# An SSM mixer stage: the carried part of y computed feature-major, with C times the decays formed on GpSimd

## The chip, the cores and the metric

The kernel runs on one core of one Trainium2 chip. The metric is the device time of one execution in microseconds. A core has TensorE (PE, with its weight loads shown as PEld), VectorE (DVE), ScalarE (ACT), GpSimd (POOL) and SyncE (SP), which run their own instruction streams and meet only at semaphores; DMA queues are fed by SP and by POOL.

## The reference, cut to what matters

The program is a two-layer block: attention and a mixture of experts, then a state-space mixer (an SSM in chunked form) and a second mixture of experts. The change touches the mixer alone. Its core, per batch element and head (64 heads of 64 features, state size 128):

```python
proj = input_states @ in_proj_w.T          # gate z, x with B and C, dt
hBC  = silu(conv1d_causal_4_taps(x, B, C) + bias)
dt   = softplus(dt + dt_bias);  Adt = -exp(A_log) * dt
A_cum = cumsum(Adt within a chunk)
Y_diag = (C @ B^T * exp(segsum(Adt))) @ (x * dt)            # inside a chunk
states = B^T @ (exp(A_cum[-1] - A_cum) * x * dt)            # of each chunk
state carried into chunk c = exp(chunk decay) * earlier state + states
Y_off[l, p] = sum_n C[l, n] * carried[p, n] * exp(A_cum[l]) # carried part
y  = Y_diag + Y_off + D * x
out = (rmsnorm(y * silu(gate)) * norm_w) @ out_proj_w.T
```

The kernel uses chunks of its own, four of 128 tokens in a batch element of 512, so three chunks have a carried part.

## The kernel before, in words

**Tiles.** The mixer loops over 4 batch elements (`GROUPS`) and, in each, 32 tiles of 128 features (two heads each): 128 tiles, one a step. Features lie on the partitions, the 512 tokens of the batch element along the free dimension. `mixer_stream` (L2063) runs the steps; a step works on five tiles at once, `tiles[0]` the newest to `tiles[4]` the oldest, so one tile passes through five steps. The order of the work on each engine is written out by hand in one function for each engine, and only semaphore waits tie them.

**One step, engine by engine, before the change.**
- TensorE (L2139 on): project x of tile 0 into PSUM (`project`, L2148, 6 matmuls); transpose the convolved x of tile 1 (L2162); for y of tile 3, transpose back the scaled carried part `y_off` (L2171) and add the inside-the-chunk products (L2176, two heads side by side in the two halves of the array); project z of tile 0 (L2148 again); state sums of tile 1 (L2189); C times states of tile 2 into bank `PO` (L2197); output projection of tile 4 (L2204).
- ScalarE: scale `PO` of tile 3 by the decays into `y_off` (L2230, 6 small instructions); eight Relu on `l_mat` of tile 1 (L2239); first tap of the convolution of tile 0 (`cv`, L2245); Exp of `l_mat` (L2251); square of tile 4 (L2256); tanh for x (`thx`, L2261) and for z (`thg`, L2266) of tile 0.
- VectorE: the carried states of tile 2, a copy (L2288) and four multiply-adds (L2293); the decay matrix times C B^T for tile 2 (L2341, both inputs in SBUF, shown as `outs<-l_mat,g_mat`); `xdt` of tile 1 out of PSUM (L2305); three taps of tile 0 (L2315); `yd` of tile 3 (L2322); the SiLU product `xc` of tile 0 (L2328, both inputs in SBUF); `sgt` of tile 0 (L2334).
- GpSimd: `xdec`, the decayed x, of tile 1 (L2368, waits for `xdt`); running sum of squares for tile 4 (L2376, shown as `gates<-gates,sq`); `yg` of tile 3 (L2383).

**What is woven in.** While batch element b is in the mixer, the routing of batch element b-1 for the second mixture of experts runs inside steps 4 to 15 of b (`route_pe`, `route_act`, `route_dve`, `route_pool`: 12 steps with extra work, called through `route(...)` at the marked places). From step 16 of b GpSimd also issues, behind its own step, scatters to HBM (`route_scatter`, L1680 to L1683: two tiny copies and an indirect DMA): two a step in four steps, then one a step in 12 steps, and one a step in the first four steps of the next b (of the drain after the last). Between two batch elements each engine runs a `between` part (the norm). This is so for b = 1, 2, 3; b = 0 has neither.

```python
for it in range(first, FT // U):
    for u in range(U):
        run(b, it, u)
        n = (it - first) * U + u
        for m in range(n + min(n, U), n + 1 + min(n + 1, U)):
            scatter(en, b - 1, m)
```

## Time and profile before

| what | value |
|---|---|
| runs shown | 2289.25, 2297.69, 2305.37 us (median 2297.69) |
| profiled execution, own time | 2296.97 us |
| its span | 2295.2 us |
| mixer steps (first to last `thx`, L2261) | 870.1 to 1931.8 us of the span |
| busy over the span | PE 1986.1, PEld 1622.4, DVE 1700.5, ACT 1461.2, POOL 973.7 us |
| steps of b = 1 with scatters, 1270 to 1410 us | PE 140.00 of 140 us, DVE 128.15, ACT 123.41, POOL 98.04; granted clock 1.00 |
| routing steps and `between`, 1140 to 1270 us | PE 117.73 of 130 us, DVE 115.00, ACT 99.89, POOL 59.91; granted clock 0.93 |

A row of the timeline gives start in us from the span's start, time in us, engine, line, operation, what is written and read, shapes, how many instructions are merged, and in brackets how long the engine was idle before it and who ended that. Instructions of ScalarE and VectorE overlap a little at their ends, so the distance between two starts is the cost of the first in a full queue, and less than its duration.

### The profile page before, as it was taken

The numbers are of one execution on the slowest core, as the hardware profiler recorded it, in microseconds if no ns is written. First come the engines' busy times: TensorE is split into PE (matmuls) and PEld (weight loads), VectorE is DVE, ScalarE is ACT, GpSimd is POOL, SyncE is SP. The second block draws the span as 40 slices with busy tenths as digits, with TensorE's granted clock in tenths as the row PEclk, the third lists the DMA queues.
The fourth block names the chain that finished last, engine by engine and source line by source line (L and its number), as shares of the span: only waits on it lengthen the run. The fifth ranks groups of instructions, "written<-read, shape, count | busy, mean of one in ns | idle before, by whom it ended". The sixth has DMA issues, their size and how long they took to land.

```text
span 2295.2 us, 40993 instructions
## 1 busy us (share of the span) xinstructions
PE 1986.1 (87%) x12211; PEld 1622.4 (71%) x12211; DVE 1700.5 (74%) x3913; ACT 1461.2 (64%) x3983; POOL 973.7 (42%) x1025
## 2 busy tenths in 40 slices
PE   4787988887699468999998998999989999689995
PEld 4566766666677256888877887878877788467772
DVE  4676766676634667999899998999989997664444
ACT  1473747465244157888887888878887887345550
POOL 0120302021177112455454765547655567177550
PEclk8799989899699779999999999999999999899998
DMA  4147383837833403444343554445534452635557
GB/s 129 38 152 295 130 350 106 338 109 282 328 97 102 147 10 138 158 154 145 127 147 125 169 175 144 142 137 171 165 137 142 146 179 93 214 117 176 162 146 272
DMA packets 143589, 372.67 MB, mean 162 GB/s; under 512 B 22256, under 2 KB 67696, under 8 KB 141072
## 3 DMA queue, kind: packets, MB, share of 16 engines
q1 hardware_dynamic: 128160, 328.39, 41.8%
q0 software_dynamic: 15216, 41.67, 5.3%
q8 instruction: 106, 1.74, 0.3%
q14 instruction: 107, 0.88, 0.1%
HBM read 232.71 MB, written 137.27 MB: 161 GB/s over the span
## 4 chain that ended last, share of the span: by engine, by line
PE 60%; DVE 17%; ACT 13%; issue 5%; DMA 2%; POOL 1%; SPq 1%; DVEq 0%; POOLq 0%; ACTq 0%
PE bank L2148 12%; PE bank L2204 6%; ACT work L701 5%; PE bank L2585 5%; PE bank L2176 4%; DVE cv L2315 3%; PE bank L2197 3%; PE bank L2189 3%; PE bank L1074 3%; PE bank L2622 2%; ACT l_mat L2239 2%; PE bank L2162 2%; DVE nmax L607 2%; PE bank L1103 2%; PE bank L775 1%
## 5 line engine op out<-in xcount | busy, mean ns | idle before, releaser
L2148 PE MATMUL bank<-h_hi,wi 128*128 128x512 f32 x1024 | 403.9, 436 | 1.3 <-ACTq L151 1.3
L2239 ACT ACTIVATE l_mat<-l_mat,cum_tok 128x128 f32<-128x128 f32 x1024 | 315.1, 424 | 0.0
L2315 DVE SCALAR_TENSOR_TENSOR cv<-bank,cw,cv 128x511 f32<-128x511 f32 (+2 forms) x384 | 287.4, 748 | 32.1 <-ACT cv L2245 13.5
L2368 POOL TENSOR_TENSOR xdec<-xdt,dec_tok 128x384 f32<-128x384 f32 x128 | 107.9, 843 | 387.6 <-DVE xdt L2305 354.4
L2383 POOL TENSOR_TENSOR yg<-yd,sgt 128x512 f32<-128x512 f32 x128 | 227.2, 1775 | 45.7 <-DVE yd L2322 45.7
L2204 PE MATMUL bank<-wo,yg 128*128 128x256 f32 x1024 | 242.5, 380 | 1.5 <-POOL yg L2383 1.5
L2148 PEld LDWEIGHTS bank<-h_hi,wi 128*128 128x128 f32 x1024 | 195.5, 191 | 62.0 <-issue 23.8
L2148 PE MATMUL bank<-h_lo,wi 128*128 128x512 f32 x512 | 203.4, 397 | 0.0
L2204 PEld LDWEIGHTS bank<-wo,yg 128*128 128x128 f32 x1024 | 185.1, 191 | 21.5 <-POOL yg L2383 1.9
L2376 POOL TENSOR_TENSOR gates<-gates,sq 128x512 f32<-128x512 f32 x128 | 164.1, 1282 | 72.0 <-ACT sq L2256 71.9
L845 POOL CAST w_hi<-w_raw 128x512 fp32r<-128x512 f32 x32 | 21.1, 659 | 392.0 <-ACTq L151 241.2
L701 ACT ACTIVATE work<-bank,nmax 128x512 f32<-128x512 f32 (+3 forms) x256 | 135.1, 535 | 68.7 <-DVE nmax L607 67.3
L2230 ACT ACTIVATE y_off<-bank,e_tok 128x64 f32<-128x64 f32 x768 | 170.8, 323 | 8.0 <-PE bank L2197 7.6
L2261 ACT ACTIVATE thx<-cv 128x512 f32<-128x512 f32 x128 | 80.8, 631 | 148.3 <-DVE cv L2315 148.3
L2341 DVE TENSOR_TENSOR outs<-l_mat,g_mat 128x1024 f32<-128x1024 f32 x128 | 157.9, 1234 | 0.0
L2693 POOL DMA_INDIRECT chosen_rows<-experts_held,experts_kept x127 | 121.5, 957 | 71.9 <-ACT experts_held L2673 57.9
L660 DVE TENSOR_TENSOR hb<-bank,pt_hi 128x512 fp32r<-128x512 f32 (+1 forms) x192 | 114.4, 600 | 50.5 <-ACT pt_hi L655 50.4
L2176 PE MATMUL bank<-outs,xdt 128*64 128x128 f32 x2048 | 144.4, 285 | 0.0
L607 DVE TENSOR_REDUCE nmax<-bank 128x1 f32<-128x512 f32 (+3 forms) x256 | 117.6, 484 | 31.2 <-PE bank L780 31.2
L2251 ACT ACTIVATE l_mat<-l_mat 128x1024 f32<-128x1024 f32 x128 | 137.3, 1073 | 0.0
L2176 PEld LDWEIGHTS bank<-outs,xdt 128*64 128x64 f32 x2048 | 112.8, 140 | 22.2 <-issue 22.2
L2293 DVE SCALAR_TENSOR_TENSOR st<-st,e_in,bank 128x64 f32<-128x64 f32 x512 | 121.0, 278 | 9.1
(419 smaller groups left out, 4947.6 us busy)
## 6 DMA issues: line engine op xcount, KB each, us to landing
sorted_rows<-blank SPq DMA_DIRECT2D x16, 4644.0 KB, 31.9
wi<-in_weights_split SPq DMA_DIRECT2D x128, 512.0 KB, 3.8
l_mat<-running_sums SPq DMA_DIRECT2D x128, 512.0 KB, 4.9
experts_got<-chosen_rows SPq DMA_DIRECT2D x32, 512.0 KB, 8.6
wo<-out_weights_normed SPq DMA_DIRECT2D x128, 128.0 KB
experts_xt<-sorted_rows SPq DMA_DIRECT2D x127, 129.0 KB, 2.3
w_raw<-in_wi SPq DMA_DIRECT2D x32, 256.0 KB, 2.7
in_weights_split<-w_hi SPq DMA_DIRECT2D x32, 256.0 KB, 2.9
```

Source lines behind the costliest of these rows:

```text
L607: last = e.tensor_reduce(nmax[:, h, q:q + 1], bank[n % 3][:, col:col + P * (q + 1)], AX.X, ALU.max, negate=True)
L701: last = e.activation(pp[:, h % 2, QOFF[q]:QOFF[q] + w], bank[u][:, col:col + w], ACT.Exp, bias=nmax[:, h, q:q + 1], accum_out=ssum[:, h, ...
L2148: mm = e.matmul(dst[:, :], l, r[:, k, tok], start=(n == 0), stop=(n == 3 * KD - 1))
L2176: mm = e.matmul(PY[rows, c * P:(c + 1) * P], xdt[:, w.four, c, rows], m_mat[:, w.two, hh, c * P:(c + 1) * P], start=False, stop=(c == NC - 1),
L2204: mm = e.matmul(token_major((bank[0], bank[1]), i), yg[:, w.two, i * P:(i + 1) * P], wo[:, w.two, :], start=False, stop=w.end, skip_group_ ...
L2230: last = e.activation(y_off[:, c, rows], PO[:, c * P + hh * SSM_P:c * P + (hh + 1) * SSM_P], ACT.Identity, scale=e_tok[:, c, hh, bass.ds(w ...
L2239: last = e.activation(part, part, ACT.Relu, bias=cum_tok[:, c, hh, bass.ds(w.g, 1)], scale=-1.0)
L2251: e.activation(l_mat[:, w.four, :, :], l_mat[:, w.four, :, :], ACT.Exp, scale=-1.0).then_inc(s_l, 1)
L2315: e.scalar_tensor_tensor(out=cv[:, w.two, n:SEQ], in0=PSX[w.two][:, 0:SEQ - n], scalar=cw[:, bass.ds(w.f, 1), TAPS - 1 - n], in1=cv[:, w.t ...
L2341: v.e.tensor_tensor(m_mat[:, w.two, :, :], l_mat[:, w.four, :, :], g_mat[:, w.b, :, :].rearrange("p c l -> p (c l)").unsqueeze(1).broadcas ...
L2376: e.tensor_tensor(sq_sum[:, w.b % 2, :], sq_sum[:, w.b % 2, :], sq[:, :], ALU.add).then_inc(s_acc, 1)
L2383: e.tensor_tensor(yg[:, w.two, :], yd[:, :], sgt[:, w.four, :], ALU.mult).then_inc(s_yg, 1)
```

## The change

The carried part of y is no longer made token-major, scaled and transposed back. ScalarE makes the exponential of the broadcast running sums for both heads (`ce`, 768 columns, tile 1) before its eight Relu, and waits for it because the Relu overwrite `l_mat`. GpSimd multiplies it by C (tile 2, right behind `xdec`), in three buffers. TensorE then adds states times `ce` to the same PSUM tile as the rest of y, six matmuls in pairs of heads; the three transposes and the three C-times-state matmuls go, with bank `PO` and `e_tok`. The first state is copied out of PSUM by ScalarE at the end of its step of tile 1, instead of by VectorE at the start of the next; VectorE waits for it (`s_first`) as well as for the state sums. The two tanh write straight into `xc` and `sgt`. On TensorE the routing work marked "p" moves behind a wait for the first tap of tile 0 (`s_cv`); on ScalarE that marked "a" comes first in the step.

```diff
--- before.py
+++ after.py
@@ -1428,14 +1427,13 @@
     start.close()
 
     cv = sb("cv", [P, 2, SEQ], where=stream)
-    thx, thg = sb("thx", [P, SEQ], where=stream), sb("thg", [P, SEQ], where=stream)
     xc = sb("xc", [P, U, SEQ], where=stream)
     sgt = sb("sgt", [P, U, SEQ], where=stream)
     l_mat = sb("l_mat", [P, U, 2, SEQ], where=stream)
     xdt = sb("xdt", [P, U, NC, P], where=stream)
     xdec = sb("xdec", [P, NC - 1, P], where=stream)
     st = sb("st", [P, 2, NC - 1, P], where=stream)
-    y_off = sb("y_off", [P, NC - 1, P], where=stream)
+    ce = sb("ce", [P, 3, 2, SEQ - P], where=stream)
     yd = sb("yd", [P, SEQ], where=stream)
     yg = sb("yg", [P, 2, SEQ], where=stream)
     sq = sb("sq", [P, SEQ], where=stream)
...
@@ -2157,7 +2154,7 @@
         w = tiles[1]
         if w.live:
             e.wait_ge(s_xc, done(w.g))
-            e.wait_ge(s_st, done(w.g - 1, 3))
+            e.wait_ge(s_st, done(w.g - 1, 2))
             for c in range(NC):
                 mm = e.transpose(PT[:, c * P:(c + 1) * P], xc[:, w.four, c * P:(c + 1) * P], ident[:, :])
             mm.then_inc(s_t, 1)
...
@@ -2165,16 +2162,20 @@
         if w.live:
             e.wait_ge(s_m, done(w.g))
             e.wait_ge(s_xdt, done(w.g))
-            e.wait_ge(s_offs, done(w.g))
+            e.wait_ge(s_ce, done(w.g))
+            e.wait_ge(s_st, done(w.g, 2))
             e.wait_ge(s_yd, done(w.g - 1))
-            for c in range(1, NC):
-                e.matmul(PY[:, c * P:(c + 1) * P], y_off[:, c - 1, :], ident[:, :], is_transpose=True, start=(c == 1),
-                         stop=False, skip_group_check=True)
             for c in range(NC):
                 for hh in range(2):
                     rows = slice(hh * SSM_P, (hh + 1) * SSM_P)
-                    mm = e.matmul(PY[rows, c * P:(c + 1) * P], xdt[:, w.four, c, rows],
-                                  m_mat[:, w.two, hh, c * P:(c + 1) * P], start=False, stop=(c == NC - 1),
+                    e.matmul(PY[rows, c * P:(c + 1) * P], xdt[:, w.four, c, rows],
+                             m_mat[:, w.two, hh, c * P:(c + 1) * P], start=(c == 0), stop=False,
+                             skip_group_check=True)
+            for c in range(1, NC):
+                for hh in range(2):
+                    rows = slice(hh * SSM_P, (hh + 1) * SSM_P)
+                    mm = e.matmul(PY[rows, c * P:(c + 1) * P], st[:, w.two, c - 1, rows],
+                                  ce[:, w.three, hh, (c - 1) * P:c * P], start=False, stop=(c == NC - 1),
                                   skip_group_check=True)
             mm.then_inc(s_y, 1)
         w = tiles[0]
...
@@ -2188,14 +2189,10 @@
             for c in range(NC - 1):
                 mm = e.matmul(PT[:, c * P:(c + 1) * P], b_tok[:, w.b, c, :], xdec[:, c, :], start=True, stop=True)
             mm.then_inc(s_ss, 1)
-        w = tiles[2]
+        w = tiles[0]
         if w.live:
-            e.wait_ge(s_st, done(w.g, 3))
-            e.wait_ge(s_offs, done(w.g - 1))
+            e.wait_ge(s_cv, done(w.g))
             route("p")
-            for c in range(NC - 1):
-                mm = e.matmul(PO[:, c * P:(c + 1) * P], c_t[:, w.b, c, :], st[:, w.two, c, :], start=True, stop=True)
-            mm.then_inc(s_off, 1)
         w = tiles[4]
         if w.live:
             e.wait_ge(s_yg, done(w.g))
...
@@ -2219,20 +2216,13 @@
 
     def mixer_act_step(a, tiles, route):
         e = a.e
-        w = tiles[3]
-        if w.live:
-            e.wait_ge(s_off, done(w.g))
-            route("a")
-            e.wait_ge(s_y, done(w.g - 1))
-            for c in range(NC - 1):
-                for hh in range(2):
-                    rows = slice(hh * SSM_P, (hh + 1) * SSM_P)
-                    last = e.activation(y_off[:, c, rows], PO[:, c * P + hh * SSM_P:c * P + (hh + 1) * SSM_P],
-                                        ACT.Identity, scale=e_tok[:, c, hh, bass.ds(w.g, 1)])
-            last.then_inc(s_offs, 1)
+        route("a")
         w = tiles[1]
         if w.live:
             e.wait_ge(s_lb[w.four], 16 + w.loaded_i)
+            e.wait_ge(s_y, done(w.g - 3))
+            e.activation(ce[:, w.three, :, :], l_mat[:, w.four, :, P:SEQ], ACT.Exp).then_inc(s_e, 1)
+            e.wait_ge(s_e, done(w.g))
             for hh in range(2):
                 for c in range(NC):
                     part = l_mat[:, w.four, hh, c * P:(c + 1) * P]
...
@@ -2257,13 +2247,18 @@
         w = tiles[0]
         if w.live:
             e.wait_ge(s_tap, done(w.g, 3))
-            e.wait_ge(s_xc, done(w.g - 1))
-            e.activation(thx[:, :], cv[:, w.two, :], ACT.Tanh, scale=0.5).then_inc(s_thx, 1)
+            e.wait_ge(s_yd, done(w.g - U))
+            e.activation(xc[:, w.four, :], cv[:, w.two, :], ACT.Tanh, scale=0.5).then_inc(s_thx, 1)
         w = tiles[0]
         if w.live:
             e.wait_ge(s_z, done(w.g))
-            e.wait_ge(s_sg, done(w.g - 1))
-            e.activation(thg[:, :], PSZ[:, :], ACT.Tanh, scale=0.5).then_inc(s_thz, 1)
+            e.wait_ge(s_yg, done(w.g - U))
+            e.activation(sgt[:, w.four, :], PSZ[:, :], ACT.Tanh, scale=0.5).then_inc(s_thz, 1)
+        w = tiles[1]
+        if w.live:
+            e.wait_ge(s_ss, done(w.g))
+            e.wait_ge(s_y, done(w.g - 2))
+            e.activation(st[:, w.two, 0, :], PT[:, 0:P], ACT.Copy).then_inc(s_first, 1)
 
     def mixer_act_between(a, b):
         e = a.e
...
@@ -2283,15 +2278,15 @@
         w = tiles[2]
         if w.live:
             e.wait_ge(s_ss, done(w.g))
+            e.wait_ge(s_first, done(w.g))
             route("a")
-            e.wait_ge(s_off, done(w.g - 2))
-            e.tensor_copy(st[:, w.two, 0, :], PT[:, 0:P]).then_inc(s_st, 1)
             for c in (1, 2):
-                e.wait_ge(s_st, done(w.g, 3) + (c - 3))
+                if c == 2:
+                    e.wait_ge(s_st, done(w.g, 2) - 1)
                 for hh in range(2):
                     cols = slice(hh * SSM_P, (hh + 1) * SSM_P)
                     last = e.scalar_tensor_tensor(out=st[:, w.two, c, cols], in0=st[:, w.two, c - 1, cols],
-                                                  scalar=e_in[:, hh, bass.ds(w.g, 1), c],
+                                                  scalar=e_in[:, hh, bass.ds(w.g, 1), c - 1],
                                                   in1=PT[:, c * P + hh * SSM_P:c * P + (hh + 1) * SSM_P],
                                                   op0=ALU.mult, op1=ALU.add)
                 last.then_inc(s_st, 1)
...
@@ -2324,14 +2319,12 @@
         w = tiles[0]
         if w.live:
             e.wait_ge(s_thx, done(w.g))
-            e.wait_ge(s_yd, done(w.g - U))
-            e.scalar_tensor_tensor(out=xc[:, w.four, :], in0=thx[:, :], scalar=1.0, in1=cv[:, w.two, :],
+            e.scalar_tensor_tensor(out=xc[:, w.four, :], in0=xc[:, w.four, :], scalar=1.0, in1=cv[:, w.two, :],
                                    op0=ALU.add, op1=ALU.mult).then_inc(s_xc, 1)
         w = tiles[0]
         if w.live:
             e.wait_ge(s_thz, done(w.g))
-            e.wait_ge(s_yg, done(w.g - U))
-            e.scalar_tensor_tensor(out=sgt[:, w.four, :], in0=thg[:, :], scalar=1.0, in1=PSZ[:, :],
+            e.scalar_tensor_tensor(out=sgt[:, w.four, :], in0=sgt[:, w.four, :], scalar=1.0, in1=PSZ[:, :],
                                    op0=ALU.add, op1=ALU.mult).then_inc(s_sg, 1)
         route("z")
 
...
@@ -2369,6 +2362,12 @@
                             xdt[:, w.four, 0:NC - 1, :].rearrange("p c (h f) -> p c h f", h=2),
                             dec_tok[:, :, :, bass.ds(w.g, 1)].broadcast_to([P, NC - 1, 2, SSM_P]),
                             ALU.mult).then_inc(s_xdec, 1)
+        w = tiles[2]
+        if w.live:
+            e.wait_ge(s_e, done(w.g))
+            e.tensor_tensor(ce[:, w.three, :, :], ce[:, w.three, :, :],
+                            c_t[:, w.b, :, :].rearrange("p c l -> p (c l)").unsqueeze(1).broadcast_to([P, 2, SEQ - P]),
+                            ALU.mult).then_inc(s_ce, 1)
         w = tiles[4]
         if w.live:
             e.wait_ge(s_sq, done(w.g))
...
```

## Rows read from the trace of the kernel before

**Rows 1.** Chain that ended last, pieces of TensorE: start us, us, what.

```profile
1304.48 0.33 PE bank L2171 x3
1304.81 1.02 PE bank L2176 x16
1308.09 0.67 PE bank L2197 x6
```

**Rows 2.** Timeline of ScalarE over one step, from `thx` to `thx`.

```profile
1307.68 0.63 ACT L2261 ACTIVATE thx<-cv 128x512 f32<-128x512 f32 x1 [0.92 <-DVE cv L2315]
...
1308.80 1.34 ACT L2230 ACTIVATE y_off<-bank,e_tok 128x64 f32<-128x64 f32 x6
...
1309.99 2.46 ACT L2239 ACTIVATE l_mat<-l_mat,cum_tok 128x128 f32<-128x128 f32 x8
...
1312.99 1.07 ACT L2251 ACTIVATE l_mat<-l_mat 128x1024 f32<-128x1024 f32 x1
...
1315.50 0.63 ACT L2261 ACTIVATE thx<-cv 128x512 f32<-128x512 f32 x1 [0.92 <-DVE cv L2315]
```

**Rows 3.** Timeline of VectorE over the same step.

```profile
1308.34 0.69 DVE L2328 SCALAR_TENSOR_TENSOR xc<-thx,cv 128x512 f32<-128x512 f32 x1
...
1309.55 0.28 DVE L2288 COPY st<-bank 128x128 f32<-128x128 f32 x1
...
1309.87 0.98 DVE L2293 SCALAR_TENSOR_TENSOR st<-st,e_in,bank 128x64 f32<-128x64 f32 x4
...
1310.76 1.22 DVE L2341 TENSOR_TENSOR outs<-l_mat,g_mat 128x1024 f32<-128x1024 f32 x1
...
1312.35 0.69 DVE L2305 TENSOR_TENSOR xdt<-bank,dt_tok 128x512 f32<-128x512 f32 x1 [0.37 <-PE bank L2162]
...
1313.15 2.31 DVE L2315 SCALAR_TENSOR_TENSOR cv<-bank,cw,cv 128x511 f32<-128x511 f32 x3
```

**Rows 4.** Timeline of GpSimd over the same step, one with a scatter.

```profile
1308.38 1.79 POOL L2383 TENSOR_TENSOR yg<-yd,sgt 128x512 f32<-128x512 f32 x1 [0.26 <-DVE yd L2322]
...
1310.11 0.19 POOL L1680 COPY freed_rows<-tw 128x1 f32<-128x1 f32 x1
...
1310.69 1.00 POOL L1683 DMA_INDIRECT sorted_rows<-freed_rows,slot_u  x1 [0.28 <-POOL freed_rows L1681]
...
1313.12 0.84 POOL L2368 TENSOR_TENSOR xdec<-xdt,dec_tok 128x384 f32<-128x384 f32 x1 [1.43 <-DVE xdt L2305]
...
1314.66 1.28 POOL L2376 TENSOR_TENSOR gates<-gates,sq 128x512 f32<-128x512 f32 x1 [0.70 <-ACT sq L2256]
```

**Rows 5.** Timeline of the mixer's drain, VectorE and GpSimd.

```profile
1939.50 1.26 POOL L2383 TENSOR_TENSOR yg<-yd,sgt 128x512 f32<-128x512 f32 x1
1939.90 1.95 DVE L2341 TENSOR_TENSOR outs<-l_mat,g_mat 128x1024 f32<-128x1024 f32 x1
1940.72 1.18 POOL L1680 COPY freed_rows<-tw 128x1 f32<-128x1 f32 x1
```

**Rows 6.** Timeline of ScalarE, a step of b = 0, early in the stream.

```profile
914.71 0.63 ACT L2261 ACTIVATE thx<-cv 128x512 f32<-128x512 f32 x1 [0.92 <-DVE cv L2315]
...
922.42 0.63 ACT L2261 ACTIVATE thx<-cv 128x512 f32<-128x512 f32 x1 [0.92 <-DVE cv L2315]
```

**Rows 7.** GpSimd's groups by form: shapes, count, busy us, mean ns, idle before.

```profile
L1186 POOL TENSOR_TENSOR experts_entries<-outs,tw 128x752 f32<-128x752 f32 x1 | 3.4, 3444 | 3.5 <-DVE outs L1307 3.5
```

**Rows 8.** ScalarE's groups by form.

```profile
L1569 ACT ACTIVATE freed_rows<-bank 128x128 f32<-128x128 f32 x4 | 1.1, 278 | 7.0 <-PE bank L2197 4.3 <-PE bank L2564 2.7
```

**Rows 9.** Chain that ended last, pieces in the routing steps of b = 1.

```profile
1203.94 0.76 PE bank L2197 x6
...
1219.51 1.91 PE bank L2176 x16
...
1229.62 0.67 DVE cv L2315
...
1238.36 0.67 DVE cv L2315
```

More of the change, by code:

```diff
@@ L2019, in start_pool @@
                                 ALU.subtract).then_inc(p_low, 1)
[L2022 removed]
+    (s_x, s_z, s_e, s_diff, s_cv, s_tap, s_thx, s_thz, s_xc, s_sg, s_l, s_m, s_t, s_xdt, s_xdec, s_ss, s_first, s_st, s_ce,
      s_y, s_yd, s_yg, s_sq, s_acc, s_o) = [sem("mix_" + n) for n in (
[L2024 to L2025 removed]
+         "x", "z", "decay_rows", "sum_diffs", "conv_first", "taps", "tanh_x", "tanh_z", "x_conv", "silu_z", "decay_mat", "m_mat",
+         "x_turned", "x_dt", "x_decayed", "state_sums", "first_state", "states", "c_decayed", "y", "y_skip", "y_gated",
          "squares", "squares_summed", "out")]
@@ L2051, in __init__ @@
             self.g = b * FT + self.f
-            self.two, self.four = f % 2, f % U
+            self.two, self.three, self.four = f % 2, self.g % 3, f % U
             self.loaded_i = 16 * (b * (FT // U) + (f // U if first else it + f // U) + 1)
@@ L2394, in mixer_pe @@
     def mixer_pe(t):
-        for s in (s_x, s_z, s_t, s_ss, s_off, s_y, s_o):
+        for s in (s_x, s_z, s_t, s_ss, s_y, s_o):
             t.e.drain().then_inc(s, BACK)
@@ L2402, in mixer_act @@
     def mixer_act(a):
-        for s in (s_cv, s_thx, s_thz, s_diff, s_l, s_sq, s_offs):
+        for s in (s_cv, s_thx, s_thz, s_e, s_diff, s_l, s_sq, s_first):
             a.e.drain().then_inc(s, BACK)
@@ L2419, in mixer_pool @@
     def mixer_pool(q):
-        for s in (s_xdec, s_yg, s_acc):
+        for s in (s_xdec, s_ce, s_yg, s_acc):
             q.e.drain().then_inc(s, BACK)
```

13 lines of the change are left out of this document (4 added, 9 removed).

## The prediction, made before the changed kernel ran

> **What bounds the kernel now.** I read the chain of waits first, then one step's timeline engine by engine, then looked for places where VectorE and GpSimd meet. In the plain steps and in those with scatters the chain names nothing but TensorE, and pieces follow each other without a gap. A step takes 7.82 us (`thx` to `thx`, 1307.68 to 1315.50) [rows 2]. The three pieces of it that the change touches are the transposes of `y_off` (0.33), the products of y (1.02) and C times states (0.67) [rows 1]. Close behind TensorE comes a second loop: taps, `thx`, `thg`, `y_off`, eight Relu, first tap, taps again, between ScalarE and VectorE. Early in b = 0, where TensorE is still ahead of it, it turns in 7.71 us with nothing else in the way [rows 6]. So whatever TensorE gains, 0.11 of it counts until this loop is shortened as well.
>
> **TensorE.** Gone are 0.33 + 0.67 = 1.00 us. New are six matmuls, 12 records, in pairs of heads like the 16 records of y. One pass of 128 columns takes 0.11 (0.33 / 3, 0.67 / 6) [rows 1]; six pair passes are 0.66, or 0.77 by y's own row (1.02 / 8, its opening gap included). I take 0.66, since the gap is paid once: 7.82 - 1.00 + 0.66 = 7.48, at most 7.59. The new wait for the first tap ahead of "p" comes long after that tap.
>
> **ScalarE.** The stretch from the first `y_off` to the first Relu, 1.19 us, goes [rows 2]. In its place stand the copy of a 128-column PSUM tile, 0.28 long and less in a full queue [rows 8], and an Exp over 768 columns, between `thx` (512 columns, 0.63) and the Exp of `l_mat` (1024, 1.07) [rows 2]: 0.85. The Relu wait for its end, so it counts in full, with 0.04 for the signal. 0.20 + 0.89 = 1.09 (bounds 1.0 and 1.17): the loop falls from 7.71 to about 7.61. The copy waits for the state sums of the same step; TensorE has these about 0.3 us before ScalarE comes to it, as long as `xdec` is in time. The waits for older y cost nothing, since those y are a step or more old or come before the state sums on TensorE. The Tanh in place saves a buffer and no time.
>
> **VectorE.** The first-state copy goes, 1309.87 - 1309.55 = 0.32 us [rows 3]. Its wait for ScalarE's copy is covered by `sgt`.
>
> **GpSimd.** The product with C is new, two SBUF inputs of 768 columns. By `xdec` (384 columns, 0.84: 2.19 ns a column) it is 1.68; by `yg` where nothing disturbs it (512, 1.26: 2.46 ns) 1.89; by a line through the two 2.10; the dearest row, 752 columns in 3.44, would make it 3.5 [rows 4, 5, 7]. I take 1.85, nearest to `yg`, which has the same plain operands. The Trainium skill, page "GPSIMD Engine Reference", section "Elementwise — side-by-side cycle accounting", has 4497 ns for 2048 columns of such an operation; scaled (an estimate) that is 1.69, and with it the loop below would be 7.60 and not 7.76.
>
> **What the averages hide: a port that the two engines share.** In the drain the decay product L2341 starts at 1939.90 while `yg` is on GpSimd until 1940.76, and takes 1.95 instead of its usual 1.22; the tiny copy L1680 behind it takes 1.18 instead of 0.19 [rows 3, 4, 5]. So the first held to 0.13 before `yg`'s end, the second to 0.14 before L2341's end. The same shows in each ordinary step: `yg` starts 0.04 after `xc` and takes 1.79, not 1.26, 0.53 of it waiting for `xc` [rows 3, 4, 5]. `xdec` and the sum of squares beside the taps are not stretched, nor is L2341 beside the indirect DMA. As a rule of this trace: L2328 (`xc`) and L2341, the two with both inputs in SBUF, and GpSimd's elementwise work exclude each other; who starts first keeps the port, and VectorE, if it waits, gets it before GpSimd's next instruction. The Trainium skill, page "SBUF — State Buffer", section "Who interferes with whom", calls it an exclusive lock, and speaks against more elementwise work on GpSimd; the trace agrees, at 0.73 us for one meeting.
>
> **Plain steps.** Count from the start of `xdt`. `xdec` starts at 0.77 [rows 3, 4], `ce` at 1.57, the sum of squares at 3.38, ending 4.66. The taps can start at 0.60 (0.69 less the 0.09 by which VectorE's neighbours overlap, as L2293 and L2341 do [rows 3]), and `xc` comes 3.01 after them (1308.34 + 7.82 - 1313.15), at 3.61. The sum of squares is on the port by then, so `xc` runs from 4.53, 0.92 late. From there 1.21 to the states, 0.89, and 1.13 for L2341 [rows 3] bring the next `xdt` at 7.76. This loop of VectorE and GpSimd is longer than ScalarE's 7.61 and TensorE's 7.48, and sets the step: 7.76, a gain of 0.06. Over the 32 steps of b = 0: -2 us.
>
> **Steps with scatters.** One scatter costs GpSimd 1.62 (1310.11 to 1311.69 and a signal) [rows 4]. With one a step GpSimd would be free at 7.93, before the next `xdec` at 8.53. With two it is free at 9.55, a full 1.0 late, and that turns the order round: now `ce` holds `xc`, `yg` holds L2341, and L2341 holds L1680. GpSimd's own round is then `xdec` 0.80, `ce` until it frees the port 1.72, `xc` 0.56, sum of squares 1.27 less 0.04, `yg` 1.26 less 0.13, L2341 1.22 less 0.14, scatter 1.62: 8.14 us. The next `xdt` is 0.8 earlier than GpSimd can take it, so GpSimd stays late when the double scatters are over: 8.14, +0.32 a step. For 20 steps a group: 20 x 0.32 + 4 x 1.62 = 12.9, less 0.8 of lateness that costs nothing, less 1.7 because a GpSimd later still meets fewer of VectorE's two (following the first six steps one by one gives 5.9, not 7.6): 10.4. Three groups, the last partly in the drain: +30 us.
>
> **Routing steps and between.** Here VectorE carries the chain; taps to taps is 8.74 [rows 9]. Each such step gets the 0.92 and loses the 0.32: +0.6, four a group. After a stall TensorE runs nearer the lower of its two clock levels (y 1.91 instead of 1.02 [rows 1, 9]), and z and `thg` wait behind y: the new passes cost 1.4 there, the transposes give back 0.66; beside the late `xc` and less 0.32 I take +0.4, four times. C times states leaves the chain once, behind the router's scores (0.76 [rows 9]): -0.8. Steps with two extra transposes stay. Together +3.2 a group, +9 us.
>
> **Sum.** -2 + 30 + 9 = +37 on the profiled execution's 2296.97, which lies 0.7 under the median of the runs: 2334 us. With `ce` from 1.68 to 2.10 the scatter steps move by -10 to +15, and routing may be off by 6: its own range is 2318 to 2355.
>
> **Rivals.**
> *GpSimd catches up.* In the late order `yg` starts 1.79 after `xc` (0.56 + 1.27 - 0.04) and L2341 is ready at 2.10 (1.21 + 0.89); if that margin of 0.3 is lost, L2341 goes first and the singles return to 7.76. Then a group costs about 3 for the doubles less 0.8, in all -2 + 6 + 9: 2311. For it: many small distances make the margin. Against: all of them are steady in the trace.
> *Faster: the port costs nothing.* Place: the meeting of the sum of squares with `xc`. If the product with C takes 1.69 or less, the loop is 7.60 and ScalarE's 7.61 decides; if the late order does not arise either, 92 steps gain 0.2 (-18) and some eight VectorE-bound steps a group 0.32 (-8): 2271. For it: `xdec`'s rate. Against: the double scatters overload GpSimd even so (8.0 a single step).
> *The product with C is dear.* At 3.5 the late round is 9.8 and plain steps pass 8.1: above 2430.
> *No pairs.* If the new matmuls run one behind the other, 12 x 0.11 = 1.32, TensorE needs 8.14 in every step: 92 x 0.32, some 2330 even without the port. Against: y's 16 records in 1.02.
>
> **How the numbers follow.** Late order 0.46; catching up 0.22; the port costs nothing 0.14; dear product 0.06; no pairs 0.04; something between, near no change, 0.08. 1% (23 us, about what can be told from no change) puts the bounds at 2275 and 2321. Slower: most of the first, the fourth and fifth, a little of the second, 0.52; faster: most of the third, 0.11; same: 0.37. The range 2278 to 2362 leaves out the dear product and the lower half of the third.
>
> **What would show it.** Right: the product with C near 1.85; `xc` recorded at about 1.6 instead of 0.69 in plain steps; steps near 7.76 in b = 0 and 8.1 behind the double scatters, with L2341 near 2 us and L1680 near 1.2; GpSimd in the chain of waits. Wrong: `xc` still 0.69 (the loop as counted is wrong), TensorE still without gaps (the new matmuls are dearer), or singles below 7.82 (GpSimd caught up).

## The result and the profile after

| | before | after |
|---|---|---|
| median of the runs | 2299.41 us (4 runs) | 2358.20 us (4 runs, 2354.64 to 2362.43) |
| span of the profiled execution | 2295.2 us | 2353.0 us |
| first to last Tanh of the mixer, 127 steps | 1061.7 us | 1120.9 us |

The change makes the kernel slower: ratio 1.026, 95% interval 1.0227 to 1.0292, 58.8 us by the medians. The forecast was 2334, +37: the right side, and over a third too small. All of the difference lies in the mixer, 59.2 us from its first Tanh to its last.

Engines as a whole, and the chain's shares, from the page of the profile after:

```profile
PE 1975.9 (84%) x12595; PEld 1580.6 (67%) x12595; DVE 1812.4 (77%) x3785; ACT 1427.4 (61%) x3470; POOL 1215.0 (52%) x1153
...
PE 43%; DVE 27%; ACT 10%; issue 10%; POOL 6%; DMA 2%; SPq 1%; DVEq 0%; POOLq 0%; ACTq 0%
...
L2322 DVE SCALAR_TENSOR_TENSOR xc<-xc,cv 128x512 f32<-128x512 f32 x128 | 248.7, 1943 | 7.2 <-ACT xc L2251 2.1
...
L2368 POOL TENSOR_TENSOR ce<-ce,c_t 128x768 f32<-128x768 f32 x128 | 235.4, 1839 | 0.0
```

The product with C takes 1.84 (its forecast was 1.85). `xc`, an operation of 0.69 when nothing disturbs it [rows 3], has a mean of 1.94: (1.943 - 0.69) x 128 = 160 us of VectorE's "busy" time are waiting. An engine shown as 77% busy is here partly an engine that stands still.

**A plain step.** VectorE, then GpSimd, in the profile after (answers to [rows 3, 4]):

```profile
935.39 1.58 DVE L2322 SCALAR_TENSOR_TENSOR xc<-xc,cv 128x512 f32<-128x512 f32 x1
...
938.37 1.22 DVE L2334 TENSOR_TENSOR outs<-l_mat,g_mat 128x1024 f32<-128x1024 f32 x1
...
943.12 1.58 DVE L2322 SCALAR_TENSOR_TENSOR xc<-xc,cv 128x512 f32<-128x512 f32 x1
```

```profile
932.54 0.84 POOL L2361 TENSOR_TENSOR xdec<-xdt,dec_tok 128x384 f32<-128x384 f32 x1 [2.15 <-DVE xdt L2300]
933.34 1.84 POOL L2368 TENSOR_TENSOR ce<-ce,c_t 128x768 f32<-128x768 f32 x1
935.15 1.27 POOL L2375 TENSOR_TENSOR gates<-gates,sq 128x512 f32<-128x512 f32 x1
936.37 1.75 POOL L2382 TENSOR_TENSOR yg<-yd,sgt 128x512 f32<-128x512 f32 x1
```

`xc` is ready at 935.39, 0.24 after the sum of squares began, and gets the port when that ends: 1.58 instead of 0.69. `yg`, started at 936.37, waits in turn for `xc`. The step is 943.12 - 935.39 = 7.73, forecast 7.76, and 7.82 before. ScalarE's row of new work (answers to [rows 2]):

```profile
935.74 0.27 ACT L2261 ACTIVATE st<-bank 128x128 f32<-128x128 f32 x1
935.89 0.85 ACT L2224 ACTIVATE ce<-l_mat 128x768 f32<-128x768 f32 x1
936.77 2.46 ACT L2229 ACTIVATE l_mat<-l_mat,cum_tok 128x128 f32<-128x128 f32 x8
```

From the copy's start to the first Relu 1.03 (forecast 1.09). In the second to ninth step of b = 0, in which the meetings of VectorE and GpSimd are still absent or short (`xc` 0.69 to 1.44), a step takes 7.54 to 7.58, except one of 8.21 in which ScalarE waits for a late TensorE. That is ScalarE's own round with VectorE, forecast 7.61. And TensorE's new pieces in the chain (answers to [rows 1]):

```profile
946.29 0.04 issue
946.33 0.63 PE bank L2159 x4
946.96 1.02 PE bank L2171 x16
947.99 0.66 PE bank L2177 x12
```

0.66 for the twelve new records, as forecast: 1.00 us of TensorE's work went and 0.66 came. The chain still names TensorE alone in plain steps, with gaps of 0.04 to 0.05, and the prediction had put that down as a sign of dearer matmuls. They are not dearer: the wait is inside the transposes, which take 0.63 in the chain, with TensorE's weight loads idle for 0.45 before them. In the chain before they took 0.44:

```profile
1311.87 0.44 PE bank L2162 x4
```

A run below (Tanh in PSUM) has the same TensorE work in a step of 7.55.

**A pair of steps with one scatter each.** VectorE and GpSimd of the profile after, b = 1, behind the double scatters:

```profile
1329.82 1.59 DVE L2322 SCALAR_TENSOR_TENSOR xc<-xc,cv 128x512 f32<-128x512 f32 x1
...
1332.81 1.22 DVE L2334 TENSOR_TENSOR outs<-l_mat,g_mat 128x1024 f32<-128x1024 f32 x1
...
1337.56 3.06 DVE L2322 SCALAR_TENSOR_TENSOR xc<-xc,cv 128x512 f32<-128x512 f32 x1
```

```profile
1329.60 1.26 POOL L2375 TENSOR_TENSOR gates<-gates,sq 128x512 f32<-128x512 f32 x1
1330.82 1.74 POOL L2382 TENSOR_TENSOR yg<-yd,sgt 128x512 f32<-128x512 f32 x1
...
1333.09 1.83 POOL L1681 DMA_INDIRECT sorted_rows<-freed_rows,slot_u  x1 [0.28 <-POOL freed_rows L1679]
1334.93 0.86 POOL L2361 TENSOR_TENSOR xdec<-xdt,dec_tok 128x384 f32<-128x384 f32 x1
1335.73 1.86 POOL L2368 TENSOR_TENSOR ce<-ce,c_t 128x768 f32<-128x768 f32 x1
1337.53 1.29 POOL L2375 TENSOR_TENSOR gates<-gates,sq 128x512 f32<-128x512 f32 x1
1338.76 1.30 POOL L2382 TENSOR_TENSOR yg<-yd,sgt 128x512 f32<-128x512 f32 x1
1339.98 0.67 POOL L1678 COPY freed_rows<-tw 128x1 f32<-128x1 f32 x1
```

Two things here stand in no row of before. The second `xc` comes 0.03 after the sum of squares began and does not get the port when that ends: `yg` follows on GpSimd with a nearly undisturbed 1.30, and `xc` does its own 0.68 of work only from 1339.94 on, 0.12 before `yg`'s recorded end (1340.06). It takes 3.06. And L1681 starts 0.28 after L2334 did and takes 1.83 instead of 1.02: it is held until about 1333.90, 0.13 before L2334's end. So the next `xdec` starts late, and with it `ce` and the sum of squares, which gets in just ahead of `xc`. The chain of waits shows the same place like this:

```profile
1337.56 0.68 DVE xc L2322
1338.23 2.31 issue
1340.54 0.67 DVE sgt L2327
```

"issue", time in which the engine waited for nothing that the profile shows, is the wait for the port. Where the chain gives such a piece behind an instruction that is too long, the other engine's timeline has the reason.

In the step that follows the starved `xc` GpSimd is not late at all; it waits 1.85 for `xdt`:

```profile
1343.92 0.84 POOL L2361 TENSOR_TENSOR xdec<-xdt,dec_tok 128x384 f32<-128x384 f32 x1 [1.85 <-DVE xdt L2300]
```

Then a step of 7.73 follows, its DMA is held again (1350.03, 1.82), and the next `xc` is starved again. Steps of this kind alternate, 7.73 and 9.21, to the end of the batch. In the twelve steps with two scatters `xc` takes 3.34 to 4.62:

```profile
1282.41 1.84 POOL L2368 TENSOR_TENSOR ce<-ce,c_t 128x768 f32<-128x768 f32 x1
1284.21 1.26 POOL L2375 TENSOR_TENSOR gates<-gates,sq 128x512 f32<-128x512 f32 x1
1285.43 1.25 POOL L2382 TENSOR_TENSOR yg<-yd,sgt 128x512 f32<-128x512 f32 x1
```

```profile
1283.68 3.56 DVE L2322 SCALAR_TENSOR_TENSOR xc<-xc,cv 128x512 f32<-128x512 f32 x1
```

It was ready during `ce`, and two more GpSimd instructions, the sum of squares and `yg`, went ahead of it.

Between Tanhs, the whole mixer, grouped from ScalarE's timelines of both profiles (first differences of the Tanh starts, summed):

| steps | before | after | difference | forecast |
|---|---|---|---|---|
| b = 0, 35 steps | 271.2 | 269.5 | -1.7 | -2 |
| routing and between, 3 x 12 steps | 117.9, 116.4, 116.5 | 119.9, 120.1, 119.3 | +8.5 | +9 |
| with scatters, 20 + 20 + 16 steps | 158.0, 156.5, 125.2 | 175.2, 174.8, 142.2 | +52.5 | +30 |
| sum | 1061.7 | 1120.9 | +59.2 | +37 |

(The table's rows leave a few tenths at rounding.) One row carries the miss.

### The profile page after: what moved, and what is told of

It is laid out like the page before. It is cut to its first block, busy times and chain, and to the rows that moved or that the text cites. A ratio compares the mean times of both kernels' runs of the same rounds, so it can differ in the third digit from the quotient of the medians.

```text
span 2353.0 us, 40993 instructions
## 1 busy us (share of the span) xinstructions
PE 1975.9 (84%) x12595; PEld 1580.6 (67%) x12595; DVE 1812.4 (77%) x3785; ACT 1427.4 (61%) x3470; POOL 1215.0 (52%) x1153
## 4 chain that ended last, share of the span: by engine, by line
PE 43%; DVE 27%; ACT 10%; issue 10%; POOL 6%; DMA 2%; SPq 1%; DVEq 0%; POOLq 0%; ACTq 0%
PE bank L2145 6%; DVE cv L2310 6%; ACT work L701 5%; PE bank L2584 5%; PE bank L2201 3%; PE bank L1074 3%; PE bank L2171 2%; DVE xc L2322 2%; PE bank L2621 2%; DVE outs L2334 2%; DVE st L2288 2%; DVE nmax L607 2%; PE bank L1103 2%; DVE sgt L2327 2%; PE bank L2159 2%
## 5 line engine op out<-in xcount | busy, mean ns | idle before, releaser
L2322 DVE SCALAR_TENSOR_TENSOR xc<-xc,cv 128x512 f32<-128x512 f32 x128 | 248.7, 1943 | 7.2 <-ACT xc L2251 2.1
L2368 POOL TENSOR_TENSOR ce<-ce,c_t 128x768 f32<-128x768 f32 x128 | 235.4, 1839 | 0.0
L2251 ACT ACTIVATE xc<-cv 128x512 f32<-128x512 f32 x128 | 80.7, 631 | 228.8 <-DVE cv L2310 228.8
L2382 POOL TENSOR_TENSOR yg<-yd,sgt 128x512 f32<-128x512 f32 x128 | 204.7, 1599 | 0.8 <-DVE yd L2317 0.8
L2159 PE MATMUL bank<-ident,xc 128*128 128x128 f32 x512 | 84.3, 289 | 107.1 <-DVE st L2288 102.4
L2334 DVE TENSOR_TENSOR outs<-l_mat,g_mat 128x1024 f32<-128x1024 f32 x128 | 162.5, 1270 | 0.0
L2159 PEld LDWEIGHTS bank<-ident,xc 128*128 128x128 f32 x512 | 56.7, 146 | 156.3 <-issue 153.6
L2171 PE MATMUL bank<-outs,xdt 128*64 128x128 f32 x2048 | 150.1, 292 | 2.5 <-issue 2.5
```

What stands on the lines that cost most here:

```text
L2159: mm = e.transpose(PT[:, c * P:(c + 1) * P], xc[:, w.four, c * P:(c + 1) * P], ident[:, :])
L2171: e.matmul(PY[rows, c * P:(c + 1) * P], xdt[:, w.four, c, rows], m_mat[:, w.two, hh, c * P:(c + 1) * P], start=(c == 0), stop=False, skip_ ...
L2322: e.scalar_tensor_tensor(out=xc[:, w.four, :], in0=xc[:, w.four, :], scalar=1.0, in1=cv[:, w.two, :], op0=ALU.add, op1=ALU.mult).then_inc( ...
L2334: v.e.tensor_tensor(m_mat[:, w.two, :, :], l_mat[:, w.four, :, :], g_mat[:, w.b, :, :].rearrange("p c l -> p (c l)").unsqueeze(1).broadcas ...
L2368: e.tensor_tensor(ce[:, w.three, :, :], ce[:, w.three, :, :], c_t[:, w.b, :, :].rearrange("p c l -> p (c l)").unsqueeze(1).broadcast_to([P ...
L2382: e.tensor_tensor(yg[:, w.two, :], yd[:, :], sgt[:, w.four, :], ALU.mult).then_inc(s_yg, 1)
```

## The experiments

The theory at this point: the loss is VectorE and GpSimd excluding each other where both inputs of VectorE's operation lie in SBUF; the product with C makes them meet. Rivals: GpSimd's added length by itself, without any exclusion; the size of the product; the later `L2334` and the scatter. Different chips ran different groups of kernels, and the kernel before took 2336 to 2338 us on two of them and 2290.5 on a third; what counts is the ratio to the kernel before on the same chip, and the step lengths, which are the same on all. A kernel that ran once has a ratio that is good to about half a per cent (some 12 us), and its step lengths and mixer time carry the verdict.

**The changed kernel again, on one of the slower chips.** No edit.

> The changed kernel unchanged, beside the others, since another chip runs them: its ratio to the kernel before should be 1.026 again, with plain steps of 7.73 and single-scatter steps alternating between 7.73 and 9.21 us.

2398.02 against 2338.34, ratio 1.0253 (1.0225 to 1.0282). Steps of 7.73, of 7.73 and 9.21 in turn, and a mixer of 1120.8 us: the pattern is no accident of one execution.

**Take `xc` off the port.** The Tanh goes into the PSUM bank that the x projection has left, and `xc` reads it there; GpSimd does the same work as in the changed kernel.

```diff
-            e.wait_ge(s_tap, done(w.g - 2, 3))
+            e.wait_ge(s_xc, done(w.g - 2))
...
-            e.activation(xc[:, w.four, :], cv[:, w.two, :], ACT.Tanh, scale=0.5).then_inc(s_thx, 1)
+            e.activation(PSX[w.two][:, :], cv[:, w.two, :], ACT.Tanh, scale=0.5).then_inc(s_thx, 1)
...
-            e.scalar_tensor_tensor(out=xc[:, w.four, :], in0=xc[:, w.four, :], scalar=1.0, in1=cv[:, w.two, :],
+            e.wait_ge(s_yd, done(w.g - U))
+            e.scalar_tensor_tensor(out=xc[:, w.four, :], in0=PSX[w.two][:, :], scalar=1.0, in1=cv[:, w.two, :],
```

> The changed kernel, but the tanh for x goes into the PSUM bank of the x projection, so that the SiLU product xc has one SBUF input and one from PSUM. Theory (GpSimd's product holds the port that xc needs): xc takes 0.69 us again, plain steps fall from 7.73 to about 7.62 (ScalarE's loop), the alternating 9.21 us steps with a scatter vanish, total about 2280 us (2270 to 2300). Rival (the new waits and the longer y on TensorE cost the time, and the late xc is only a symptom): about 2358 us, no change.

2332.91 against 2336.37, ratio 0.9992 (0.9978 to 1.0006), where the changed kernel stands at 1.0253. GpSimd and VectorE in a plain step:

```profile
1052.56 1.85 POOL L2368 TENSOR_TENSOR ce<-ce,c_t 128x768 f32<-128x768 f32 x1
1054.38 1.27 POOL L2375 TENSOR_TENSOR gates<-gates,sq 128x512 f32<-128x512 f32 x1
1055.61 1.29 POOL L2382 TENSOR_TENSOR yg<-yd,sgt 128x512 f32<-128x512 f32 x1
```

```profile
1055.32 0.69 DVE L2322 SCALAR_TENSOR_TENSOR xc<-bank,cv 128x512 f32<-128x512 f32 x1
```

`xc` runs from 1055.32 inside the sum of squares (until 1055.65) in 0.69, and `yg` beside it in 1.29. GpSimd's length alone costs a plain step nothing: 7.55, and 7.67 with one scatter. That settles the mechanism of the plain steps and of those with one scatter. But the expected 2280 us (ratio 0.992, at most 1.000) was reached only at the upper end of its range: of each four steps with two scatters one takes 8.0 to 8.4 and three 9.2. There GpSimd has more than a step's work of its own, and L2334, which still has both inputs in SBUF, is now the one that waits, 2.37 to 3.04 instead of 1.22:

```profile
1312.13 3.01 DVE L2334 TENSOR_TENSOR outs<-l_mat,g_mat 128x1024 f32<-128x1024 f32 x1
```

**Move the product to VectorE, behind L2334.**

```diff
+            e.wait_ge(s_e, done(w.g))
+            e.tensor_tensor(ce[:, w.three, :, :], ce[:, w.three, :, :],
+                            c_t[:, w.b, :, :].rearrange("p c l -> p (c l)").unsqueeze(1).broadcast_to([P, 2, SEQ - P]),
+                            ALU.mult).then_inc(s_ce, 1)
```

(and the same lines out of GpSimd's step.)

> The changed kernel, but C times the decays is made by VectorE right behind the decay matrix product instead of by GpSimd. Theory: xc no longer meets GpSimd's sum of squares; VectorE's own round is then 6.85 + 0.93 = 7.78 us, which binds in plain and scatter steps alike; total about 2300 us (2290 to 2315). Rival (TensorE and ScalarE parts of the change cost the time): VectorE has more work, so slower than 2358 us.

2351.01, ratio 1.0049 (1.0020 to 1.0079): within the expected range, which ends at 1.007. The same 768 columns take VectorE 0.95, and `xc` is back at 0.69:

```profile
1055.40 0.69 DVE L2326 SCALAR_TENSOR_TENSOR xc<-xc,cv 128x512 f32<-128x512 f32 x1
...
1058.63 0.95 DVE L2297 TENSOR_TENSOR ce<-ce,c_t 128x768 f32<-128x768 f32 x1
```

Plain steps and those with one scatter are 7.71, steps with two 7.71 and 9.00 in turn, but the routing groups take 120.9, 121.2 and 120.5, 3.0 to 4.8 more than before, since VectorE carries the chain there and has 0.95 more to do. The longest `xc` of all is 1.99, although the scatter's DMA is held here as well, for 1.82 to 1.89 in 48 places of the mixer and in every step with one scatter: with the product gone, GpSimd has the room to be late. A held DMA does not lengthen a step by itself.

**Half the product.** One head of two is multiplied by C.

```diff
-            e.tensor_tensor(ce[:, w.three, :, :], ce[:, w.three, :, :],
-                            c_t[:, w.b, :, :].rearrange("p c l -> p (c l)").unsqueeze(1).broadcast_to([P, 2, SEQ - P]),
-                            ALU.mult).then_inc(s_ce, 1)
+            e.tensor_tensor(ce[:, w.three, 0, :], ce[:, w.three, 0, :],
+                            c_t[:, w.b, :, :].rearrange("p c l -> p (c l)"), ALU.mult).then_inc(s_ce, 1)
```

> The changed kernel, but GpSimd multiplies only one of the two heads by C (384 columns instead of 768; the other head's carried part stays without C). Theory: the product takes 0.95 us, the sum of squares is off the port about when xc is ready, plain steps near 7.62, scatter steps no longer alternate; total about 2285 us (2270 to 2305). Rival (the waits, not the port): 2358 us.

2323.4 against 2336.37, ratio 0.9945, as expected. The product takes 1.02 and plain steps 7.55, those with one scatter too; only the doubled ones stay long, at 8.9 to 9.25. So outside the doubled steps the loss hangs on some 0.8 us of GpSimd work ahead of the sum of squares: with it, the sum of squares is on the port when `xc` comes, without it, it is over.

**First state back on VectorE.**

```diff
-            e.activation(st[:, w.two, 0, :], PT[:, 0:P], ACT.Copy).then_inc(s_first, 1)
...
+            e.wait_ge(s_y, done(w.g - 2))
+            e.tensor_copy(st[:, w.two, 0, :], PT[:, 0:P]).then_inc(s_first, 1)
```

> The changed kernel, but VectorE copies the first state out of PSUM at the start of its step, as before the change. Theory (the loop of VectorE and GpSimd sets the step): 0.3 us more in VectorE's part of the loop, plain steps 8.0 instead of 7.73, total 2358 + about 30 = 2388 us (2375 to 2400). Rival (ScalarE's loop or TensorE sets the step): unchanged within 5 us, or a little faster since ScalarE's round is 0.17 shorter.

2395.61, ratio 1.0254: not the 30 us more that were expected. Plain steps did get 0.32 longer, 8.05. But the steps with one scatter are 8.05 as well, every one: the alternation is gone, and their mean falls from 8.47 to 8.05. The rows say why; GpSimd, then VectorE:

```profile
1367.59 1.01 POOL L1681 DMA_INDIRECT sorted_rows<-freed_rows,slot_u  x1 [0.28 <-POOL freed_rows L1679]
1369.54 0.84 POOL L2358 TENSOR_TENSOR xdec<-xdt,dec_tok 128x384 f32<-128x384 f32 x1 [0.94 <-DVE xdt L2297]
```

```profile
1364.32 1.58 DVE L2319 SCALAR_TENSOR_TENSOR xc<-xc,cv 128x512 f32<-128x512 f32 x1
...
1366.42 0.28 DVE L2278 COPY st<-bank 128x128 f32<-128x128 f32 x1
...
1367.63 1.22 DVE L2331 TENSOR_TENSOR outs<-l_mat,g_mat 128x1024 f32<-128x1024 f32 x1
```

The copy puts the decay product 0.04 behind the start of the scatter's DMA instead of 0.28 ahead of it. The DMA takes its 1.01, GpSimd idles 0.94 before `xdec`, and is not late. Taking the copy off VectorE is worth 0.32 in each plain step and costs 0.42 in each with one scatter, since it brings the decay product ahead of the DMA: a saving on the path that makes a collision elsewhere. (What the DMA does to the step after it is read from these rows; the copy's place changed more than the DMA.)

**Before, with a product that nobody reads.** The kernel before, Tanhs in place, and on GpSimd behind `xdec` one product of 768 columns. First with C times C:

```diff
+            c_wide = c_t[:, w.b, :, :].rearrange("p c l -> p (c l)").unsqueeze(1).broadcast_to([P, 2, SEQ - P])
+            e.tensor_tensor(extra[:, :, :], c_wide, c_wide, ALU.mult).then_inc(s_extra, 1)
```

> The kernel before with both tanh written in place (to make room) and, behind xdec on GpSimd, an unused product of the same size as C times the decays (768 columns). Nothing else of the change is in it. Theory (the product on the shared port is what costs): plain steps 7.76 + 0.32 for the first-state copy on VectorE = 8.05 us, scatter steps 8.1 to 9.2, ratio 1.03 to 1.04. Rival (the loss comes from the new dependences between engines): as before, 7.82 us a step and a ratio of 1.00.

2372.03 against 2338.34, 1.0144; plain steps stay 7.82, the expected 8.05 was missed. The cause is in its row: this product takes 1.47, not 1.84. Then with two tiles as inputs:

```diff
+            e.tensor_tensor(extra[:, :, :], extra[:, :, :],
+                            c_t[:, w.b, :, :].rearrange("p c l -> p (c l)").unsqueeze(1).broadcast_to([P, 2, SEQ - P]),
+                            ALU.mult).then_inc(s_extra, 1)
```

> As e6 (the kernel before, both tanh in place, an unused product on GpSimd behind xdec), but the product now has the operands of the change: a tile of 768 columns multiplied in place by C, since e6's, with both inputs from C, took only 1.47 us and left plain steps at 7.82. Theory (the round of VectorE and GpSimd, 7.73 measured in the changed kernel, plus 0.32 for the first-state copy): plain steps 8.05 us, the product 1.84 us, ratio to the kernel before 1.035 (1.025 to 1.045). Rival (the round is not what sets the step): 7.82 us a plain step, 1.014 as e6.

2356.31 against 2290.53, 1.0287, and the step is 8.05, as expected. The product's row in the first kernel, then in the second:

```profile
L2375 POOL TENSOR_TENSOR extra<-c_t 128x768 f32<-128x768 f32 x128 | 187.8, 1467 | 0.0
```

```profile
L2378 POOL TENSOR_TENSOR extra<-extra,c_t 128x768 f32<-128x768 f32 x128 | 235.1, 1837 | 0.2
```

So the loss needs nothing of the change but the product: the kernel before, its other work as it was except for the two Tanhs' places, is slower by 2.9% with it, one run against one, and its mixer takes 1117.1 us instead of 1061.7, which is 2.4% of the execution. The changed kernel's is 1120.9: all the rest of the change (TensorE, ScalarE, the moved copy) brings nothing as long as the product lies where it does.

**Sum of squares ahead of the product.**

```diff
+            e.tensor_tensor(sq_sum[:, w.b % 2, :], sq_sum[:, w.b % 2, :], sq[:, :], ALU.add).then_inc(s_acc, 1)
             e.tensor_tensor(ce[:, w.three, :, :], ce[:, w.three, :, :],
...
-            e.tensor_tensor(sq_sum[:, w.b % 2, :], sq_sum[:, w.b % 2, :], sq[:, :], ALU.add).then_inc(s_acc, 1)
```

> The changed kernel, but GpSimd adds the squares before it multiplies by C, so that xc meets the longer product. Theory (who starts first on the port keeps it): the product runs from 3.3 to 5.1 us after xdt, xc is held to 5.0, plain steps 8.2 us instead of 7.73; ratio near 1.04. Rival (xc is late for another reason): plain steps stay at 7.73.

2411.16 against 2338.34, 1.0311: worse than the change, as expected, though by less: plain steps of 7.76 and 8.05 in turn, not 8.2. `xc` now meets the product:

```profile
1050.79 1.84 POOL L2373 TENSOR_TENSOR ce<-ce,c_t 128x768 f32<-128x768 f32 x1
```

```profile
1051.28 1.90 DVE L2322 SCALAR_TENSOR_TENSOR xc<-xc,cv 128x512 f32<-128x512 f32 x1
```

Held for 1.21, until 0.14 before the product's end, and then it is served, ahead of `yg`. The order of GpSimd's work moves the loss by a few tenths a step; it doesn't remove it.

**Split: the product on VectorE in the four steps with two scatters, on GpSimd elsewhere.**

```diff
+    def doubled(w):
+        return w.b >= 1 and 14 <= w.f <= 17
...
+        if w.live and doubled(w):
+            e.wait_ge(s_ce, done(w.g - 1))
+            e.wait_ge(s_e, done(w.g))
+            e.tensor_tensor(ce[:, w.three, :, :], ce[:, w.three, :, :],
+                            c_t[:, w.b, :, :].rearrange("p c l -> p (c l)").unsqueeze(1).broadcast_to([P, 2, SEQ - P]),
+                            ALU.mult).then_inc(s_ce, 1)
...
-        if w.live:
+        if w.live and not doubled(w):
+            e.wait_ge(s_ce, done(w.g - 1))
```

> The changed kernel with one edit: VectorE makes C times the decays in the four steps with two scatters, GpSimd in all others; the tanh stays in SBUF. Theory: GpSimd's load in the doubled steps is one part of the loss and the meeting with xc another; the doubled steps fall from 9.75 to about 8.3 us, single-scatter steps go on alternating between 7.73 and 9.21, total 3 x 6 = 18 us less than the changed kernel, ratio to the kernel before 1.018 (1.015 to 1.021). Rival (once GpSimd is not late after the doubles, the singles stay at 7.73): 3 x 10 more, ratio 1.003 to 1.008.

2344.42 against 2290.53, 1.0235, outside the expected 1.015 to 1.021. But that is one run against one: the mixer takes 1102.1 us, 18.8 less than in the changed kernel where 18 was expected, and 40.4 more than before, which would be 1.018. The other 13 us lie outside the mixer, where the two kernels do the same. The doubled steps get shorter (9.00, 7.71, 8.13, 9.97), yet the single ones go on alternating 7.73 and 9.21. The prediction said of them that they inherit their lateness from the double scatters. The last of the doubled steps is still long here, so this run alone would not refute it; with the row above, in which GpSimd stands idle for 1.85 and the pattern goes on, it falls.

**Both: Tanh in PSUM and the split.** The edits of the Tanh in PSUM and of the split, together and unchanged.

> The tanh for x in PSUM, as in e1, and C times the decays made by VectorE in the four steps with two scatters and by GpSimd in all others. Theory (GpSimd's load and the port are the whole loss): the four doubled steps fall from 9.23 to about 7.9 us each, three groups of them save 15 us against e1; plain 7.55, single-scatter steps 7.67; ratio to the kernel before about 0.990 (0.985 to 0.995). Rival (something else than GpSimd's load makes the doubled steps long): as e1, 0.999.

2319.41 against 2338.34, ratio 0.9916 (0.9893 to 0.9939): 0.8% faster than the kernel before, 3.3% faster than the changed kernel, the lowest ratio of all tried. Plain steps 7.55, single scatters 7.55 to 7.71, doubled 7.55 to 7.67, mixer 1036.4 against 1061.7 us. 7.55 is the length that the new ScalarE round has alone; with both collisions gone, the change's other parts bring what they save.

| kernel | product with C | plain step | one scatter | two scatters | mixer, us | ratio to before |
|---|---|---|---|---|---|---|
| before | none | 7.82 | 7.82 | 7.82 | 1061.7 | 1 |
| changed | GpSimd 1.84 | 7.73 | 7.73, 9.21 | 9.5 to 11.0 | 1120.9 | 1.026 |
| Tanh in PSUM | GpSimd 1.84 | 7.55 | 7.67 | 8.0 to 9.2 | 1052.5 | 0.9992 |
| product on VectorE | VectorE 0.95 | 7.71 | 7.71 | 7.71, 9.00 | 1073.1 | 1.0049 |
| one head | GpSimd 1.02 | 7.55 | 7.55 | 8.9 to 9.25 | 1043.8 | 0.9945 |
| first state on VectorE | GpSimd 1.84 | 8.05 | 8.05 | 8.4 to 10.3 | 1117.4 | 1.0254 |
| split only | by step | 7.73 | 7.73, 9.21 | 7.7 to 10.0 | 1102.1 | 1.0235 |
| PSUM and split | by step | 7.55 | 7.55 to 7.71 | 7.55 to 7.67 | 1036.4 | 0.9916 |

The mixer column is from one profile of each kernel; the kernel before has one on one chip alone.

## Why the prediction was right, and where it fell short

The direction was right, and so was the mechanism of the plain steps. That 2358 lies in the stated range of 2278 to 2362 is in part luck: it is 4 us from the range's end and beyond the 2318 to 2355 that the prediction worked out for its own account, and the "late order" from which it took most of its loss is not what the kernel does.

**TensorE, ScalarE, the product's price: right.** 0.66 for the carried passes, 1.84 for 1.85, `xc` at 1.58 for about 1.6, ScalarE's round 7.55 for 7.61; GpSimd, 1% of the chain of waits before, is 6% of it. The Trainium skill's page "GPSIMD Engine Reference", section "Elementwise — side-by-side cycle accounting", would have made the product 1.69 by its figure for 2048 columns (an estimate); the row of this kernel's own `yg`, scaled to 1.89, was nearer.

**Plain steps: right, with the mechanism.** 7.73 for 7.76, and b = 0 gives back 1.7 us for 2. The loop from `xdt` over `xdec`, `ce` and the sum of squares to `xc` is what sets the step: take `xc` off the port and the step is 7.55, though GpSimd does the same.

**Routing and between: right in its sum.** +8.5 for +9. Step by step the differences run from -0.9 to +1.1 (for b = 2), so the sum's fit does not bear out each of its terms. One term can be read by itself: the new passes do cost more behind a stall, 1.28 instead of 0.66 in the chain, for the 1.4 that was counted; the granted clock is 0.65 in this stretch:

```profile
1252.45 1.40 PE bank L2171 x16
1253.86 1.28 PE bank L2177 x12
```

**Steps with scatters: the step that failed,** +52.5 for +30. Two halves:

*Double scatters.* The forecast had each at 8.14 + 1.62 = 9.76, and four of the kernel's (those of b = 1) are 10.76, 9.71, 9.75 and 9.74. The length of three in four is right. What failed were the deductions, 0.8 for lateness that costs nothing and 1.7 for meetings that a late GpSimd avoids: 2.5 a group, 7.5 in all, and none of it appeared. The counting had `xc` served at the end of `ce`; in the twelve steps it waits through the sum of squares and `yg` too, 3.34 to 4.62 in all. And the first of each four is 1.0 to 1.2 longer than forecast. The twelve steps cost 26 us instead of 23.3 - 7.5 = 15.8.

*Single scatters.* Forecast 8.14 each, +0.32; measured 7.73 and 9.21 in turn, mean 8.47, +0.65. Over 38 such steps that is 24.7 us instead of 12.2. Two sentences of the prediction carry this. The first, "VectorE, if it waits, gets it before GpSimd's next instruction", is wrong in every second of these steps: there `xc` waits through the sum of squares and through `yg`, and pays about 1.5 more than in the step before. The second, "nor is L2341 beside the indirect DMA" stretched, was true of the row it came from and says less than I read into it. It is not the product that is stretched but the DMA, and only if the product starts first. The late order that I derived (`yg` holds L2341, L2341 holds the copy) is not what the steps settle into; in them L2334 keeps its 1.22, where "near 2" was named as a sign, and in every second one holds the DMA behind it.

The remaining 1.8 of the 52.5 are the first steps of each group, where the routing ends.

**What took the place of the deductions is shown by three runs.** With the first state back on VectorE the DMA starts first, is not held, and no `xc` is starved in a step with one scatter. With `xc` off the port, singles are 7.67. With the product out of the doubled steps, the singles alternate as before. That the DMA is held by the decay product is read from the rows: in the changed kernel's mixer it takes 1.82 to 1.86 in all 23 places where the decay product started first and 0.98 to 1.02 in the 49 others. The other kernels have no exception either (1.71 to 2.00 against at most 1.23), but no run changed that alone. And the link from the held DMA to the starved `xc` needs the product with C on GpSimd too: without it, or with half of it, the DMA is held in every step with one scatter, and no such step is longer than a plain one.

**The rivals.** "The port costs nothing" is refuted by the Tanh in PSUM, worth 2.6%. "No pairs" and "the product is dear" are refuted by 0.66 and 1.84. "GpSimd catches up" was half right: every second single step is indeed back at 7.73, and the step after it pays.

**What stays open.** Which engine gets the port when GpSimd goes from one instruction to the next. `xc` that came 0.24 after the sum of squares began was served at its end; one that came 0.03 after was not, but waited through `yg`. An `xc` that came during `ce` was served at its end in one place and in the doubled steps was not. Near the end of the mixer the decay product shows that arriving well after a start doesn't help always; GpSimd, then VectorE, profile after:

```profile
1995.49 1.26 POOL L2375 TENSOR_TENSOR gates<-gates,sq 128x512 f32<-128x512 f32 x1
1996.72 1.26 POOL L2382 TENSOR_TENSOR yg<-yd,sgt 128x512 f32<-128x512 f32 x1
```

```profile
1996.08 3.01 DVE L2334 TENSOR_TENSOR outs<-l_mat,g_mat 128x1024 f32<-128x1024 f32 x1
```

It came 0.59 after the sum of squares began and waited through `yg`. So it is not how late VectorE comes. What does sort the meetings with the sum of squares in the changed kernel's trace is whether `yg`'s input `yd` was ready when the sum of squares began: in all 31 places where it was (by 0.01 to 1.58), `yg` went ahead of the waiting `xc`; in the 86 where `yd` ended 0.14 or more after that start, `xc` was served first. L2334 at 1996.08 fits as well (`yd` ready 1.36 before). This is read from rows and not tested. It is also not the whole rule: for an `xc` that comes during `ce`, `sq` was ready beforehand in places of both kinds, and in other runs (one head, the unread product) `yg` also went ahead with `yd` 0.15 to 0.38 late.

The section of the Trainium skill that the prediction names for the port (page "SBUF — State Buffer", "Who interferes with whom") states the lock; advice against elementwise work on GpSimd does not stand in that section.

## What to carry to other kernels

Before elementwise work goes to an idle GpSimd, list VectorE's instructions that have both inputs in SBUF, and follow one whole round of both engines with the new instruction in it: what counts is what GpSimd has running when such an instruction comes, not GpSimd's share of the span. Then bound a meeting from both sides: the better case is the rest of one GpSimd instruction, the worse is every instruction that GpSimd has queued back to back. The remedy that worked was to move one input of VectorE's instruction to PSUM, which cost nothing here, since a bank was free at that time (`xc` takes 0.69 either way), and to put the product on the other engine just in the steps in which GpSimd is full.
